# A step's opening re-ordered on four engines: key and query projections ahead of the probabilities' transposes, and the inverse root split around the head outputs

## The reference, cut to what matters

```
def attn_layer(x, Wqkv, qs, ksc, Wo):              # 16 heads of 64, windows of 32
    q, k, v = jnp.split(x @ Wqkv, 3, -1)            # x is 128 wide, INNER is 1024
    q = l2norm(q) * qs
    k = l2norm(k) * ksc
    q = q * cos * scale + rotate_half(q) * sin * scale
    k = k * cos * inv + rotate_half(k) * sin * inv
    out = local_attention(q, k, v)                  # each window sees itself and the one before
    return out @ Wo
def ffn_layer(x, g, bln, W1, b1, W2, b2):
    xn = (x - mu) / jnp.sqrt(var + 1e-05) * g + bln
    a, gate = jnp.split(xn @ W1 + b1, 2, -1)
    return a * gelu(gate) @ W2 + b2
for i in range(6):
    x = attn_layer(shift_tokens(x), ...) + x
    x = ffn_layer(shift_tokens(x), ...) + x
```

## Time and profile before

| | us |
|---|---|
| median of 3 runs | 2012.22 |
| lowest and highest | 2008.62, 2013.55 |
| the profiled execution | 2012.52 |
| its span (first to last instruction) | 2010.7 |
| first and last projection of a query (L1280) | 198.3, 1930.4 |
| TensorE, VectorE, ScalarE, GpSimd busy | 1805.9, 1557.0, 1164.3, 1455.2 |

### The profile page before, as it was taken

One profiled execution on the slowest core, in us unless ns is written; L12 is line 12 of the kernel. 1 busy time (PEld: TensorE's weight loads), 2 busy tenths in 40 slices (PEclk: granted clock), 3 DMA queues, 4 the chain that ended last, 5 costly groups with the idle time before them and its releaser, 6 DMA issues. The chain is left out here.

```text
span 2010.7 us, 85596 instructions
## 1 busy us (share of the span) xinstructions
PE 1805.9 (90%) x34280; PEld 1311.9 (65%) x34280; DVE 1557.0 (77%) x2776; ACT 1164.3 (58%) x1966; POOL 1455.2 (72%) x967
## 2 busy tenths in 40 slices
PE   7774689999999999999999999999999999999995
PEld 3453466676776666766666666667676667676764
DVE  4764688887888878888788788887887888878864
ACT  2311356666666666666666666666666666666662
POOL 3221688877887778777877787778777877787771
PEclk9875899999999999999999999999999999999997
DMA  4000122223222223222223322233222232222220
GB/s 151 2 3 1 44 65 65 59 54 86 73 70 53 55 63 91 59 70 63 61 53 84 77 68 55 52 82 81 63 58 59 63 86 63 70 63 55 55 58 22
DMA packets 93581, 123.43 MB, mean 61 GB/s; under 512 B 27760, under 2 KB 41808, under 8 KB 93392
## 3 DMA queue, kind: packets, MB, share of 16 engines
q1 hardware_dynamic: 93232, 122.42, 24.2%
q10 hardware_dynamic: 288, 0.13, 0.0%
HBM read 20.74 MB, written 1.05 MB: 11 GB/s over the span
## 5 line engine op out<-in xcount | busy, mean ns | idle before, releaser
L999 POOL TENSOR_TENSOR across<-unit,turns 128x1024 f32<-128x1024 f32 x192 | 497.4, 2591 | 279.7 <-issue 268.4
L1006 POOL TENSOR_TENSOR rotated<-along,across 128x1024 f32<-128x1024 f32 x192 | 496.7, 2587 | 14.2
L1151 DVE TENSOR_REDUCE sums<-squares 128x16 f32<-128x1024 f32 x192 | 234.2, 1220 | 173.2 <-ACT squares L1054 173.1
L1247 PE MATMUL turn<-identity,rotated 128*128 128x128 f32 x1536 | 205.2, 277 | 36.4 <-POOL rotated L1006 36.4
L1247 PEld LDWEIGHTS turn<-identity,rotated 128*128 128x128 f32 x1536 | 172.6, 141 | 98.9 <-issue 83.4
L1032 POOL TENSOR_TENSOR along<-unit,turns 128x1024 f32<-128x1024 f32 x96 | 228.3, 2378 | 0.0
L1352 PE MATMUL proj_a<-w_qkv,shift_a 128*128 128x512 f32 x384 | 189.9, 617 | 36.4 <-DVE unit L1176 30.1
L1113 ACT COPY val<-proj_a 128x1024 f32<-128x1024 f32 x96 | 97.2, 1013 | 181.3 <-PE proj_a L1352 181.3
L1377 PEld LDWEIGHTS att<-o_t,w_o 128*128 128x128 f32 x1536 | 188.0, 193 | 6.1 <-issue 1.0
L1377 PE MATMUL att<-o_t,w_o 128*128 128x128 f32 x1536 | 188.3, 276 | 0.0
L1280 PE MATMUL proj_a<-w_qkv,shift_a 128*128 128x512 f32 x384 | 183.5, 601 | 4.3 <-POOL shift_a L988 3.0
(11 more groups left out here) (203 smaller groups left out, 3445.2 us busy)
## 6 DMA issues: line engine op xcount, KB each, us to landing
v_win<-val SPq DMA_DIRECT2D x1536, 64.0 KB, 2.0
w_qkv<-wqkv_dram SPq DMA_DIRECT2D x18, 512.0 KB, 3.8
w_o<-wo_dram SPq DMA_DIRECT2D x6, 512.0 KB, 4.6
where<-positions_dram SPq DMA_DIRECT2D x1, 2048.0 KB, 11.4
w_ffn<-ffn_dram SPq DMA_DIRECT2D x12, 170.5 KB, 2.3
w_ffn<-ffn_dram SPq DMA_DIRECT2D x6, 192.0 KB, 2.3
x_tok<-x_dram SPq DMA_DIRECT2D x4, 256.0 KB, 4.3
out_dram<-final SPq DMA_DIRECT2D x4, 256.0 KB, 2.4
```

The lines of the kernel that those rows point to most:

```text
L999: pool.tensor_tensor(a[:, :, ::-1, :], u, table, ALU.mult).then_inc(acrossed[j], 1)
L1006: pool.tensor_tensor(rotated[j][:, :, :], along[j][:, :, :], across[j][:, :, :], ALU.add).then_inc(rotated_in[j], 1)
L1151: dve.tensor_reduce(sums[:, j, :], squares[j][:, :, :], AX.X, ALU.add).then_inc(summed[j], 1)
L1247: mm = pe.transpose(bank[:, TILE * (i % 4):TILE * (i % 4) + TILE], buffer[:, TILE * i:TILE * i + TILE], identity[:, :])
```

## The change

It moves instructions and adds none. On TensorE the eight transposes of the probabilities go from ahead of the two projections to behind them. On ScalarE the two squares go ahead of the two copies `p_t`. On VectorE the inverse root is cut: its first four operations (L88 to L94) go directly behind the sums of squares, `heads_out` follows, and the last five (L96 to L104) stay behind `heads_out`. Nothing changes on GpSimd and on the DMA queue, and each wait moves with its instruction.

```
--- before.py
+++ after.py
@@ -1067,15 +1067,15 @@
                             after(act, gated, NC_ * h)
                             act.activation(gelu[0:size, i, :], up_out(i)[0:size, TWO:], ACT.Gelu,
                                            bias=w_ffn[0:size, F_B1G + i:F_B1G + i + 1]).then_inc(gelued, 1)
+                    if live["p"]:
+                        square(0)
+                        square(1)
                     if live["b"]:
                         for j in range(2):
                             act.wait_ge(p_turned, 2 * b + j + 1)
                             after(act, mixed, 2 * b)
                             act.copy(p_t[:, 4 * j:4 * j + 4, :], bank_s[:, j, :].rearrange("p (a t) -> p a t", t=TILE))\
                                 .then_inc(p_laid, 1)
-                    if live["p"]:
-                        square(0)
-                        square(1)
                     if live["a"]:
                         for j in range(2):
                             act.wait_ge(q_turned, 2 * a + j + 1)
@@ -1195,15 +1195,20 @@
                     if live["p"]:
                         sum_squares(0)
                         sum_squares(1)
+                    def root(ops):
+                        inverse_root(dve, ops, sums[:, :, :], sums_min[:, :, :], inv_norm[:, :, :],
+                                     [w[:, :, :] for w in root_work], magic[:, :, :], rooted, ROOT_OPS * p)
+
+                    if live["p"]:
+                        dve.wait_ge(summed[0], p + 1)
+                        dve.wait_ge(summed[1], p + 1)
+                        after(dve, united[1], p)
+                        root(range(0, 4))
                     if live["b"]:
                         divide_out(0)
                         divide_out(1)
                     if live["p"]:
-                        dve.wait_ge(summed[0], p + 1)
-                        dve.wait_ge(summed[1], p + 1)
-                        after(dve, united[1], p)
-                        inverse_root(dve, range(ROOT_OPS), sums[:, :, :], sums_min[:, :, :], inv_norm[:, :, :],
-                                     [w[:, :, :] for w in root_work], magic[:, :, :], rooted, ROOT_OPS * p)
+                        root(range(4, ROOT_OPS))
                         unite(0)
                         unite(1)
                     if live["a"]:
@@ -1265,12 +1270,6 @@
                                            normed[:, :], start=True, stop=True)
                         mm.then_inc(widened, 1)
 
-                    if live["b"]:
-                        pe.wait_ge(weighed, 2 * b + 2)
-                        after(pe, xb_ready, b)
-                        stand_alone(pe, passed)
-                        for j in range(2):
-                            transposes(bank_s[:, j, :], probs_flat, j, p_turned)
                     if live["p"]:
                         pe.wait_ge(shifted, 2 * p + 2)
                         pe.wait_ge(q_in, (layer_of(p) + 1) * 16)
@@ -1295,6 +1294,12 @@
                             mm = pe.matmul(bank_b[:, half, :], shift_a[mine][:, :], w_qkv[:, base:base + 512],
                                            start=True, stop=True)
                         mm.then_inc(k_projected, 1)
+                    if live["b"]:
+                        pe.wait_ge(weighed, 2 * b + 2)
+                        after(pe, xb_ready, b)
+                        stand_alone(pe, passed)
+                        for j in range(2):
+                            transposes(bank_s[:, j, :], probs_flat, j, p_turned)
                     if live["a"]:
                         pe.wait_ge(rotated_in[0], a + 1)
                         after(pe, centred, 2 * a)
```

More of the change, by code:

```diff
@@ L1266, in widen @@
                         mm.then_inc(widened, 1)
[L1268 to L1273, removed]
                     if live["p"]:
```

## The result

The changed kernel takes 2118.92 us (median of 4 runs, 2118.06 to 2123.71), the kernel before 2012.88 in the same comparison; the ratio is 1.0535 with a 95% interval of 1.0512 to 1.0558. It is slower by 5.3%, 106 us. The forecast was 2119.

The account below looks back on a forecast made before the run. TensorE was taken to set the pace. A pair of steps was to go from 36.49 to 38.82 us (36.30 + 0.81 + 1.71), adding 106 us to 2012.5: 2118.8 us, likeliest 2119, range 2040 to 2150.

Parts of the forecast that it names:

- Parts 1 and 2: TensorE's opening and ScalarE's order: q's projection starts 0.28 us earlier a pair; late copies make the mixing wait about 0.4.
- 4b: VectorE's `along` in even steps comes second to GpSimd's q `rotated`, delaying k's projection by 1.71 us in each odd step.
- Part 3: Divided root on VectorE, if nothing holds it: values' projection no longer set by `unit`; pair 36.30 us, gain 0.19.
- 4a: The root's first operations on VectorE are held by GpSimd in even steps, delaying `heads_out`: cost 0.81 us each.
- The sum: TensorE's time for an odd and an even step: 36.30 + 0.81 + 1.71 = 38.82 us, 2.33 more a pair.
- (A): Only VectorE's root is held, `along` still goes first: 0.62 us a pair, 2041 us; chance 12%.
- (B): Only VectorE's `along` is held, the root finds GpSimd idle: 1.52 us a pair, 2082 us; chance 13%.
- (C): Neither VectorE's root nor `along` is held, the ordering gains its 0.19 us a pair: 2003 us; chance 7%.
- (D): Nothing moves, since gains and the new waits on `p_t` cancel: 2012 us; chance 4%.
- (E): The clock falls below full and everything is dearer still: above 2150 us; chance 4%.

Follow-up runs that it names:

- late_along_even_whole: The changed kernel with `along` of even steps issued behind the next step's three `hidden`, and the root undivided in even steps: 2021.92 us, ratio 1.0046.

## Why the prediction was right, point by point

**Parts 1 and 2.** The q projection starts without waiting for `xb` (1029.60 + 0.50 against 1029.97 leaves no gap). k's projection in the even step is 1.80 behind the start (1.72 said), in the odd step 3.63 by 4b. The mixing is G + 4.24 and G + 4.14 instead of G + 3.96, so its wait was about 0.5 instead of 0.4: the release from ScalarE took 0.25, where I took 0.05 from VectorE's row.

**Part 3.** The values' projection has lost its gap, and V is H + 4.30 and H + 4.28 (4.22 and 4.34). That the change would be worth only 0.19 a pair if nothing were held was never seen undisturbed. The nearest run, late_along_even_whole, is 0.20 above before and not 0.19 below, but its undivided root makes the even step wait 0.28 for `unit`. Less that, an estimate is 0.08 below before, so the term was optimistic by about 0.1 a pair, within what separates two executions.

**4a.** Said: L88 ends 0.05 behind `rotated` at S + 7.13, `heads_out` at S + 8.30. Measured: S + 7.17 and S + 8.36. **4b.** Said: GpSimd first by 0.50, `along` to S + 0.69, k's projection at S + 3.53. Measured: by 0.46, 1011.38 is S + 0.74, and S + 3.63. Removal gives 1.77 for 4b. For 4a it gives 0.35, not 0.81: the unheld head outputs started at S + 7.68 and not at S + 7.49, since the mixing is 0.2 late without any hold, and the undivided root gave 0.28 back. As a price of the hold alone 0.81 was about 0.13 too high.

**The sum.** Said 38.82 for a pair; the shown pair is 38.82, the mean over the layers 38.79. This agreement to the hundredth has luck in it. It is read from an execution of 2123.71 us; one at the median of 2118.92 would have about 0.10 less a pair (an estimate, 4.8 us over 47.5 pairs). And errors cancel: the mixing is 0.2 later in each step, but where `heads_out` follows the mixing the odd step's mixing itself ran shorter (1.48 instead of 1.61, and `heads_out` 1.49 behind it instead of 1.81), and behind V the odd step is 5.67 instead of 5.81.

**The rivals.** (A) and (B) are each ruled out by rows: `along` went second and the root was held. (C) needed neither to be held; `along` with 2.98 us and L88 with 1.08 speak against it. (D) needed gains and waits to cancel, and the pair is 2.3 us longer. The clock (E) stayed at full with TensorE 89% busy.

## What to carry to other kernels

Moving small operations of one engine ahead on a queue is free only if nothing on the way can stop them. Here VectorE's 0.2 us operations stand behind a 2.4 us operation of GpSimd, and everything queued behind them stands too; so put them where GpSimd is idle, and ask of each speed-up which operation of a partner it starts earlier and what that one will hold. When an operation is moved up to the point where it "just fits", count the cover that the old place gave: 0.87 us of it hid the gating before and would have hidden half of term 4b here.

## What was new about the hardware

The order of two starts 0.2 us apart decided 1.7 us a pair: GpSimd's 2.35 us and VectorE's 1.22 us operation exclude each other in all rows read here. The one that came second ended behind the first by 0.13 to 0.15 us less than its own time: `along` of VectorE by 1.08 to 1.09 us, `rotated` and `across` of GpSimd by 2.21 to 2.24, a root operation of 0.19 us by 0.04 to 0.06. A float32 tensor_scalar of 128x32 elements was held 1.10 us just like the two-input form, while a reciprocal from SBUF to SBUF and the reductions ran beside GpSimd at their full speed.

TensorE's mixing started 0.23 to 0.25 us behind the copies of ScalarE in the steps shown, where matmuls behind VectorE's operations took 0.06 to 0.14. These are different matmuls, and over the whole trace the mixing's delay runs from 0.14 to 0.27, so that ScalarE as such is the cause is not shown.
